# A wavelet mixer and gated feed-forward on one core: gate and up handed over separately, the low half of h on GpSimd, x1 halves and 1/den moved by DMA

## The chip, the cores and the metric

The kernel runs on one core of a Trainium2 chip. The metric is the device time of one execution in microseconds (us). TensorE is called PE here, its weight loads PEld, VectorE DVE, ScalarE ACT, GpSimd POOL, and SyncE, which issues all of the kernel's DMAs, SP.

## The reference

The input is x of shape [2, 4096, 512] in f32. Two layers follow each other:

```
l, h   = two levels of depthwise 4-tap convolutions with stride 2   (analysis)
q      = elu(l2) + 1, k = q, v = l2, 16 heads of 32 channels
low    = (q @ kv) / (q @ sum(k) + 1e-6)                             (attention)
low    = two levels of repeat by 2 and depthwise 4-tap convolutions (synthesis)
r      = x + layer_norm(x + low) * gamma + beta
x1     = layer_norm(r)
h      = silu(x1 @ wg.T) * (x1 @ wu.T)      wg, wu: [1536, 512] int32 / 127
out    = layer_norm(x1 + h @ wd.T)          wd:     [512, 1536] int32 / 127
```

## The kernel before, in words

**Work and order.** A batch's 4096 tokens are taken 1024 at a time, so there are 8 iterations of 1024 tokens. The analysis of the first batch and the casting of the weights come first (about 120 us), then the synthesis and first norms of tokens 0 to 511 (`FIRST_MIX`, `FIRST_NORM`, up to 203 us), then the 8 iterations. Iterations 0 to 2 also carry the analysis of the second batch.

**The feed-forward.** An iteration has two blocks, b = 0 and 1, of 512 tokens. PE computes in f32 accuracy with f16 operands: x1 and h are split into a high and a low half in f16. In a block, k = 0 to 11 are steps of one 128-wide piece of the hidden size: `gate_up` issues 8 gate and 8 up matmuls of 512 columns into `ps_gu[k % 2]`; ACT writes silu(gate) to `gate_s` (L754); DVE multiplies it with up into `h_f` (L1070); ACT copies `h_f` to f16 `h_hi` (L758); DVE writes `h_lo = h_f - h_hi` (L1076). Then t = 0 to 3 (slots 12 to 15) are `down` for 128 tokens each: 24 matmuls into `ps_d[t % 2]` (L539, L540). DVE adds x1 into z (L1088), POOL and ACT take turns for the mean and variance (L839, L741, L816 to L821), ACT normalises (L746, semaphore `out_done`), and SP stores (L409). The product of `ps_down` may be overwritten two t later only after L1088.

**What lies beside it.** Every engine's program is a list in order, and an engine waits in that order. The table `BESIDE`, written by hand, says which steps stand in which slot (b, k), on every engine that has a part of them. On ACT the order in a slot is silu(k), the "early" steps, the copy to `h_hi`, the "late" steps (`norm1q`, `normq`, `normx`). On DVE it is L1070, the beside steps, L1076. POOL has only the beside steps in slots 0 to 11. In slots 12 to 15 POOL runs the beside steps and then the statistics of z for t; ACT runs early steps, square(t-1), late steps, normalise(t-1).

**The steps of one tile of 128 tokens**, t = 0 to 7: `xbeta` (POOL, x + beta, L790, f32, 512 wide); `norm1` (PE transposes of `s_chan`, L489; ACT copy with sum, L666; POOL mean, L795); `norm1q` (ACT square, L671; POOL L803 and L806); `norm2` (DVE L1006 and L1012; POOL mean, L810); `normq` (ACT square, L677; POOL L816, L819, L821); `normx` (ACT, x1 in f32, L683); `norm3` (four PE transposes of x1 into `ps_y`, L507; ACT writes `x1_hi`, L688; DVE writes `x1_lo`, L1020). Tiles 0 to 3 of the next iteration stand in slots (1,9) to (1,15.5), tiles 4 to 7 of this one in (0,0) to (0,11). The first gate matmul of a block waits for `x1_hi_ready` and `x1_lo_ready` of its four tiles.

**Attention.** `dens` puts q @ sum(k) for 16 heads into 16 partitions of `ps_y`; DVE adds eps and takes the reciprocal (L935, L937). `attend` for each of four channel groups multiplies a 16-partition 0/1 matrix `spread` with 1/den on PE (L473), multiplies q with kv (L474), ACT copies the spread 1/den (L661), DVE multiplies (L941).

**SP's queue.** SP issues the loads of `xt` after `norm2` (L340), the output stores in slots 12 to 15, and a few large transfers. `hold` is a wait in that queue.

The waits that tie PE to the others are, in `gate_up`:

```python
                pe.wait_ge(h_mul, NH * B + k + 1)
                for g in range(2):
...
                mm.then_inc(gu_ready, 1)
```

so that both banks of step k wait for the product of step k-2 (`h_mul` starts at 2), and ACT's silu waits for the last up matmul.

## Time and profile before

| | |
|---|---|
| median of 3 runs | 1384.56 us (1384.21 to 1386.04) |
| span of the profiled execution, first to last instruction | 1382.5 us |
| the profiled execution's own time | not given apart from its span; the runs shown are 0.1 to 0.3% longer than that span |
| PE, DVE, ACT, POOL busy | 90%, 71%, 50%, 27% of the span |
| mean granted clock of PE | 0.971 of full speed (2.4 GHz) |
| DMA | 95.2 MB, 20.8% of the 16 DMA engines' time |
| from the first gate matmul to the end | 203.0 to 1382.5 us |

How to read it: the page gives each engine's busy time. Matmuls are pipelined, so the cost of one is read from the distance between two starts in the timeline and not from its duration. Engines that are not the bottleneck may be idle at no cost; what matters is which of them PE waits for.

### The profile page before, as it was taken

To read this page: it belongs to the slowest core of one execution; us is meant where nothing else is said; L and a number is where in the kernel's file an instruction comes from. 1 tells how busy PE (TensorE), PEld (TensorE's weight loads), DVE (VectorE), ACT (ScalarE), POOL (GpSimd) and SP (SyncE) were. 2 spreads that over 40 slices of the span, in tenths; PEclk is the share of its full clock that TensorE was granted. 3 is DMA by queue.
4 is the path that set the end of the run, shared out by engine and by line. 5 is a ranking of instruction groups with operands and counts; after the bars stand their busy time and mean duration, and the time that the engine had idled before them with its cause. 6 is when DMAs were issued, how large, how long until landed. Compare 5 with 4: busy or idle time off the path is not lost.

```text
span 1382.5 us, 18903 instructions
## 1 busy us (share of the span) xinstructions
PE 1245.5 (90%) x5920; PEld 629.5 (46%) x5920; DVE 988.1 (71%) x1913; ACT 688.8 (50%) x1384; POOL 373.0 (27%) x790
## 2 busy tenths in 40 slices
PE   3997039998999989998999999999999999999998
PEld 3885025444444444444544444444444444444443
DVE  2677938988688958988489738883898478854332
ACT  2663046345753466346753466346634664365432
POOL 2001033133423044223413143304321341234101
PEclk9998559999999999999999999999999999999999
DMA  8963033000520014000500041002200130010000
GB/s 262 285 238 123 0 123 108 23 24 24 176 77 31 0 55 147 20 23 24 176 16 31 8 148 30 31 1 84 100 23 8 53 122 23 15 38 24 16 16 31
DMA packets 48465, 95.20 MB, mean 69 GB/s; under 512 B 8448, under 2 KB 25088, under 8 KB 47376
## 3 DMA queue, kind: packets, MB, share of 16 engines
q1 hardware_dynamic: 48400, 94.42, 20.8%
q8 instruction: 30, 0.49, 0.1%
q14 instruction: 35, 0.29, 0.1%
HBM read 69.21 MB, written 25.19 MB: 68 GB/s over the span
## 4 chain that ended last, share of the span: by engine, by line
DVE 29%; PE 27%; issue 22%; ACT 12%; POOL 9%; SPq 0%; DMA 0%; DVEq 0%; POOLq 0%; ACTq 0%
DVE s_chan L864 6%; DVE h_f L1070 5%; DVE low L864 5%; PE ps_down L540 3%; PE ps_down L539 3%; PE ps_gate L522 3%; PE ps_gate L523 3%; PE ps_up L523 3%; PE ps_up L522 3%; DVE hid L1076 3%; POOL rs L819 3%; DVE h_mem L864 3%; PE ps_down L572 2%; ACT junk L671 2%; DVE l L864 2%
## 5 line engine op out<-in xcount | busy, mean ns | idle before, releaser
L522 PE MATMUL ps_gate<-x_hi,w 128*128 128x512 f16 x768 | 292.4, 381 | 27.5 <-DVE h_f L1070 25.4
L539 PE MATMUL ps_down<-w,hid 128*128 128x512 f16 x768 | 292.1, 380 | 0.1
L540 PE MATMUL ps_down<-w,hid 128*128 128x512 f16 x768 | 292.1, 380 | 0.0
L523 PE MATMUL ps_gate<-x_lo,w 128*128 128x512 f16 x768 | 292.0, 380 | 0.0
L522 PE MATMUL ps_up<-x_hi,w 128*128 128x512 f16 x768 | 291.1, 379 | 0.0
L523 PE MATMUL ps_up<-x_lo,w 128*128 128x512 f16 x768 | 291.1, 379 | 0.0
L758 ACT ACTIVATE hid<-h_f 128x512 f16<-128x512 f32 x192 | 121.0, 630 | 203.2 <-DVE h_f L1070 203.2
L1070 DVE SCALAR_TENSOR_TENSOR h_f<-ps_up,gate_s 128x512 f32<-128x512 f32 x192 | 131.7, 686 | 123.7 <-ACT gate_s L754 123.1
L1076 DVE TENSOR_TENSOR hid<-h_f,hid 128x512 f16<-128x512 f32 x192 | 139.3, 725 | 57.7 <-ACT hid L758 56.8
L754 ACT ACTIVATE gate_s<-ps_gate 128x512 f32<-128x512 f32 x192 | 112.1, 584 | 70.0 <-PE ps_up L523 69.8
L522 PEld LDWEIGHTS ps_gate<-x_hi,w 128*128 128x128 f16 x768 | 75.2, 98 | 124.9 <-DVE h_f L1070 42.2
L522 PEld LDWEIGHTS ps_up<-x_hi,w 128*128 128x128 f16 x768 | 75.2, 98 | 90.8 <-issue 0.3
L523 PEld LDWEIGHTS ps_up<-x_lo,w 128*128 128x128 f16 x768 | 75.1, 98 | 90.8 <-issue 0.3
L790 POOL TENSOR_TENSOR xt<-xt,beta_b 128x512 f32<-128x512 f32 x64 | 90.1, 1429 | 97.6 <-DMA xt<-x_tok 96.8
L539 PEld LDWEIGHTS ps_down<-w,hid 128*128 128x128 f16 x768 | 75.3, 98 | 86.8 <-DVE z L1088 3.5
L540 PEld LDWEIGHTS ps_down<-w,hid 128*128 128x128 f16 x768 | 75.3, 98 | 85.2 <-issue 1.1
L864 DVE SCALAR_TENSOR_TENSOR s_chan<-low,coef,s_chan 128x512 f32<-128x512 f32 x160 | 111.5, 748 | 1.1
L523 PEld LDWEIGHTS ps_gate<-x_lo,w 128*128 128x128 f16 x768 | 75.3, 98 | 78.7 <-issue 0.8
L795 POOL TENSOR_TENSOR rs<-rs,minus_part 128x1 f32<-128x1 f32 x64 | 21.2, 331 | 324.6 <-ACT x L666 324.6
L1020 DVE TENSOR_TENSOR x_lo<-ps_y,x_hi 128x512 f16<-128x512 f32 x64 | 43.9, 687 | 85.2 <-ACT x_hi L688 85.2
L746 ACT ACTIVATE z<-z,rs 128x512 f32<-128x512 f32 x64 | 52.0, 812 | 83.3 <-POOL rs L821 83.3
L741 ACT ACTIVATE junk<-z,rs 128x512 f16<-128x512 f32 x64 | 46.0, 718 | 89.9 <-POOL rs L839 89.9
(106 smaller groups left out, 1803.8 us busy)
## 6 DMA issues: line engine op xcount, KB each, us to landing
xa<-x_chan SPq DMA_DIRECT2D x32, 515.0 KB, 5.6
xb<-x_chan SPq DMA_DIRECT2D x8, 2060.0 KB, 8.9
xt<-x_tok SPq DMA_DIRECT2D x64, 256.0 KB, 2.6
out<-z SPq DMA_DIRECT2D x64, 256.0 KB, 2.0
hid<-weights SPq DMA_DIRECT2D x12, 768.0 KB, 6.7
q_in<-q_scratch SPq DMA_DIRECT2D x8, 518.0 KB, 8.5
h_in<-h_scratch SPq DMA_DIRECT2D x8, 518.0 KB, 9.5
h_scratch<-h SPq DMA_DIRECT2D x8, 512.0 KB, 9.2
```

What stands on the lines that cost most here:

```text
L522: pe.matmul(ps_gu[k % 2][g][:, :], w, x1_hi[:, b, c, :], start=(c == 0), stop=False)
L523: mm = pe.matmul(ps_gu[k % 2][g][:, :], w, x1_lo[:, b, c, :], start=False, stop=(c == NC - 1))
L539: pe.matmul(ps_d[t % 2][:, :], h_hi[:, k, t * P:(t + 1) * P], w, start=(k == 0), stop=False)
L540: mm = pe.matmul(ps_d[t % 2][:, :], h_lo[:, k, t * P:(t + 1) * P], w, start=False, stop=(k == NH - 1))
L741: nc.scalar.activation(junk[:, :], z[:, t, :], ACT.Square, bias=rs3[:, t, 1:2], accum_out=rs3[:, t, 2:3]).then_inc(z_squares, 1)
L746: nc.scalar.activation(z[:, t, :], z[:, t, :], ACT.Identity, bias=rs3[:, t, 5:6], scale=rs3[:, t, 4:5]).then_inc(out_done, 1)
L754: nc.scalar.activation(gate_s[:, k % 2, :], ps_gu[k % 2][0][:, :], ACT.Silu, scale=WSCALE / X1_SCALE).then_inc(silu_done, 1)
L758: nc.scalar.activation(h_hi[:, k, :], h_f[:, k % 2, :], ACT.Copy).then_inc(hi_done, 1)
L790: nc.gpsimd.tensor_tensor(xt[:, t % 4, :], xt[:, t % 4, :], beta_b[:, :], ALU.add).then_inc(x_beta, 1)
L864: return V.scalar_tensor_tensor(out=acc, in0=src, scalar=coef[:, c, n:n + 1], in1=acc if add is None else add, op0=ALU.mult, op1=ALU.add)
L1070: V.scalar_tensor_tensor(out=h_f[:, k % 2, :], in0=ps_gu[k % 2][1][:, :], scalar=WSCALE * H_SCALE / X1_SCALE, in1=gate_s[:, k % 2, :], op0 ...
L1076: V.tensor_tensor(h_lo[:, k, :], h_f[:, k % 2, :], h_hi[:, k, :], ALU.subtract).then_inc(lo_done, 1)
```

## The change

Four things are changed together.

1. **Hand-overs.** Gate and up have semaphores of their own (`gate_ready`, `up_ready`). ACT's silu waits for gate alone. PE's gate matmuls of step k wait for the silu of step k-2, its up matmuls for the product of step k-2. `gate_s` is gone: silu is written to a ring of four `h_f`, and the product is formed in place.
2. **h_lo on POOL.** DVE's L1076 becomes a POOL `tensor_tensor` of f32 and f16 to f16, 128x512, in every slot 0 to 11, between POOL's early step (`norm1`) and its late ones. The silu of step k waits for `lo_done` of step k-4, and PE's `down` for `lo_done`.
3. **x1 halves by DMA.** `normx` writes the high half in f16 from x1 on ACT first, then x1; POOL subtracts (`x1_lo`, also 128x512); `norm3` is now two `dma_start_transpose` of 128x512 f16 on SP, and PE's transposes, L688 and L1020 are gone. The halves lie in the memory of `xt`, so the next load of `xt` (`reload`) waits on SP for both transposes. The step stands one to two slots earlier or later, as the table shows; on SP it is behind the store of the slot before.
4. **1/den by DMA.** `dens` writes 4 heads of each channel group to partitions 32c to 32c+3 (rows 4 to 31 are of no use), DVE takes the reciprocal over 128 partitions, SP stores `den` to DRAM, waits, and loads it with a broadcast of each row to 32 partitions for the four groups. `spread` on PE and ACT's copy L661 are gone.

```diff
+    (0, 3): [(NOW, "normx", 5), (LATE, "turn", 2), (LATE, "turn", 3), (NOW, "norm3", 4)],
+    (0, 4): [(LATE, "kv", 0), (LATE, "blocks", 0), (NOW, "norm3", 5), (NOW, "reload", 4), (NOW, "xbeta", 6),
+             (NEXT, "high1", 0)],
+    (0, 5): [(NOW, "reload", 5), (NOW, "norm1", 6), (NOW, "norm1q", 6), (NOW, "xbeta", 7)],
...
+    (0, 8): [(NOW, "normx", 7), (NOW, "norm3", 6), (NEXT, "dens", 0)],
+    (0, 9): [(NOW, "norm3", 7), (NOW, "reload", 6)],
...
+    (1, 12): [(NEXT, "normx", 1), (NEXT, "norm2", 2), (NEXT, "normq", 2), (ANA, "band2", 3), (NEXT, "norm3", 0)],
     (1, 12.5): [(NEXT, "norm1", 3), (NEXT, "norm1q", 3)],
+    (1, 13): [(NEXT, "norm3", 1), (NEXT, "reload", 0), (NEXT, "normx", 2), (NEXT, "norm2", 3), (NEXT, "normq", 3)],
+    (1, 14): [(NEXT, "norm3", 2), (NEXT, "reload", 1), (NEXT, "normx", 3)],
+    (1, 15): [(NEXT, "reload", 2), (NEXT, "norm3", 3), (NEXT, "reload", 3)],
...
 @block.sync
+            def norm3(j, batch, t):
+                b, u = t // DSUB, t % DSUB
+                if not first(j):
+                    hold(sp, up_ready, NH * (2 * j + b - 1))
+                for w, (x1_part, ready) in enumerate(((x1_hi, x1_hi_ready), (x1_lo, x1_lo_ready))):
+                    hold(sp, ready, SUBS * j + t + 1)
+                    sp.dma_start_transpose(x1_part[:, b, :, u * P:(u + 1) * P], x1_tok[:, u, w, :]
+                                           ).then_inc(x1_turned[w][u], 16)
+            def reload(j, batch, t):
...
+                for w in range(2):
+                    hold(sp, x1_turned[w][t % DSUB], 16 * (2 * j + t // DSUB + 1))
                 load_xt(j + (t + 4) // SUBS, (t + 4) % SUBS)
+            def dens(j, batch, _):
+                hold(sp, den_step, 2 * (j + 1))
+                sp.dma_start(den_dram[:, :], den[:, :]).then_inc(st_den, 16)
+                hold(sp, st_den, 16 * (j + 1))
+                for c in range(NC):
+                    rows = den_dram[c * HEAD:c * HEAD + CHUNK_HEADS, :]
+                    sp.dma_start(att[:, c, :], rows[:, None, :].to_broadcast([CHUNK_HEADS, HEAD, QW])
+                                 ).then_inc(ld_att[c], 16)
 @block.tensor
-                pe.matmul(ps_y[:, 0:QW], spread[:, c, :], den[:, :], start=True, stop=True)
...
             def gate_up(B, b, k):
-                pe.wait_ge(h_mul, NH * B + k + 1)
                 for g in range(2):
+                    pe.wait_ge((silu_done, h_mul)[g], NH * B + k + 1)
...
-                mm.then_inc(gu_ready, 1)
+                    mm.then_inc((gate_ready, up_ready)[g], 1)
 @block.scalar
             def normx(j, batch, t):
+                nc.scalar.activation(x1_tok[:, t % DSUB, 0, :], x1[:, t, :], ACT.Identity, bias=rs2[:, t, 5:6],
+                                     scale=rs2[:, t, 4:5]).then_inc(x1_hi_ready, 1)
...
-                        act.wait_ge(gu_ready, NH * B + k + 1)
-                        nc.scalar.activation(gate_s[:, k % 2, :], ps_gu[k % 2][0][:, :], ACT.Silu,
+                        act.wait_ge(gate_ready, NH * B + k + 1)
+                        act.wait_ge(lo_done, NH * B + k + 1)
+                        nc.scalar.activation(h_f[:, k % RING, :], ps_gu[k % 2][0][:, :], ACT.Silu,
...
 @block.gpsimd
+            def normx(j, batch, t):
+                n = SUBS * j + t + 1
+                pool.wait_ge(x1_ready, n)
+                pool.wait_ge(x1_hi_ready, n)
+                nc.gpsimd.tensor_tensor(x1_tok[:, t % DSUB, 1, :], x1[:, t, :], x1_tok[:, t % DSUB, 0, :],
+                                        ALU.subtract).then_inc(x1_lo_ready, 1)
...
                     for k in range(NH + DSUB):
-                        beside(b, k, i, batch, analysis, last, steps)
+                        beside(b, k, i, batch, analysis, last, early)
+                        if k < NH:
+                            pool.wait_ge(hi_done, NH * (2 * i + b) + k + 1)
+                            nc.gpsimd.tensor_tensor(h_lo[:, k, :], h_f[:, k % RING, :], h_hi[:, k, :], ALU.subtract
+                                                    ).then_inc(lo_done, 1)
+                        beside(b, k, i, batch, analysis, last, late)
 @block.vector
-                        dve.wait_ge(hi_done, n + 1)
-                        V.tensor_tensor(h_lo[:, k, :], h_f[:, k % 2, :], h_hi[:, k, :], ALU.subtract
-                                        ).then_inc(lo_done, 1)
```

## Rows read from the trace of the kernel before

**Rows 1.** The page: span and busy time, share, instructions
```profile
span 1382.5 us, 18903 instructions
...
PE 1245.5 (90%) x5920; PEld 629.5 (46%) x5920; DVE 988.1 (71%) x1913; ACT 688.8 (50%) x1384; POOL 373.0 (27%) x790
```

**Rows 2.** Windows, iterations 0 and 5: length, busy PE, PEld, DVE, ACT, POOL, clock, DMA
```profile
203.00:358.60 155.60, 147.17 (x697) 70.45 (x698) 126.38 (x246) 81.88 (x168) 47.36 (x91) 0.98 0.16 50
...
959.50:1103.90 144.40, 139.63 (x665) 66.15 (x665) 106.47 (x195) 73.77 (x152) 43.45 (x96) 1.00 0.15 51
```

**Rows 3.** Timeline of PE, a transpose and matmuls: start, duration, what
```profile
254.76 0.27 PE L507 MATMUL ps_y<-ident,x 128*128 128x128 f32 x1
254.87 0.38 PE L522 MATMUL ps_gate<-x_hi,w 128*128 128x512 f16 x1
255.09 0.38 PE L523 MATMUL ps_gate<-x_lo,w 128*128 128x512 f16 x1
```

**Rows 4.** Timeline of PE, one `attend` in iteration 5
```profile
1168.88 0.70 PE L473 MATMUL ps_y<-den,spread 16*128 16x259 f32 x2
1169.51 0.70 PE L474 MATMUL ps_x<-q_in,kv_blocks 128*128 128x259 f32 x2
```

**Rows 5.** Groups of instructions by line: busy us, mean ns, idle before, releaser
```profile
L1076 DVE TENSOR_TENSOR hid<-h_f,hid 128x512 f16<-128x512 f32 x192 | 139.3, 725 | 57.7 <-ACT hid L758 56.8
...
L790 POOL TENSOR_TENSOR xt<-xt,beta_b 128x512 f32<-128x512 f32 x64 | 90.1, 1429 | 97.6 <-DMA xt<-x_tok 96.8 <-issue 0.8
...
L1020 DVE TENSOR_TENSOR x_lo<-ps_y,x_hi 128x512 f16<-128x512 f32 x64 | 43.9, 687 | 85.2 <-ACT x_hi L688 85.2
```

**Rows 6.** Line L790 by itself: duration in ns, least, median, most
```profile
L790 POOL TENSOR_TENSOR xt<-xt,beta_b x64: 1262/1276/1858, 117.1 to 1267.3; 128x512 f32<-128x512 f32 x64
```

**Rows 7.** Timeline of POOL and DVE at the same time, iteration 6
```profile
1182.44 4.19 POOL L790 TENSOR_TENSOR xt<-xt,beta_b 128x512 f32<-128x512 f32 x3
...
1184.00 1.49 DVE L1076 TENSOR_TENSOR hid<-h_f,hid 128x512 f16<-128x512 f32 x1 [0.70 <-ACT hid L758]
```

**Rows 8.** Timeline of ACT, slots (1,9) to (1,15) of iteration 5
```profile
1070.54 0.60 ACT L754 ACTIVATE gate_s<-ps_gate 128x512 f32<-128x512 f32 x1 [0.16 <-PE ps_up L523]
...
1078.68 0.72 ACT L677 ACTIVATE junk<-x,rs 128x512 f16<-128x512 f32 x1 [1.56 <-POOL rs L810]
...
1096.91 0.80 ACT L683 ACTIVATE x<-x,rs 128x512 f32<-128x512 f32 x1
...
1101.56 0.81 ACT L746 ACTIVATE z<-z,rs 128x512 f32<-128x512 f32 x1 [1.28 <-POOL rs L821]
```

**Rows 9.** Timeline of POOL in the same slots
```profile
1077.28 0.58 POOL L803 TENSOR_SCALAR rs<-rs 128x1 f32<-128x1 f32 x1 [1.41 <-ACT junk L671]
...
1079.66 0.19 POOL L816 TENSOR_SCALAR rs<-rs 128x1 f32<-128x1 f32 x1 [1.01 <-ACT junk L677]
...
1080.56 0.19 POOL L821 TENSOR_TENSOR rs<-rs 128x1 f32<-128x1 f32 x1
```

**Rows 10.** Timeline of PE where the next block begins
```profile
1103.82 0.39 PE L522 MATMUL ps_gate<-x_hi,w 128*128 128x512 f16 x1 [0.16 <-issue]
```

**Rows 11.** Timeline of SP: start and issue time of one DMA
```profile
1110.30 0.83 SPq L337 DMA_DIRECT2D h_in<-h_scratch  x1
```

**Rows 12.** DMA issues: count, KB each, us from issue to landing
```profile
xt<-x_tok SPq DMA_DIRECT2D x64, 256.0 KB, 2.6
out<-z SPq DMA_DIRECT2D x64, 256.0 KB, 2.0
...
h_in<-h_scratch SPq DMA_DIRECT2D x8, 518.0 KB, 9.5
```

**Rows 13.** Windows: the first 3.5 us of iteration 0, PE alone
```profile
202.90:206.40 3.50, 3.46 (x9) 0.51 0.32 111
```

**Rows 14.** Timeline before iteration 0: attention, then the first gate matmul
```profile
128.24 0.43 DVE L941 TENSOR_TENSOR att<-ps_x,att 128x259 f32<-128x259 f32 x1 [2.90 <-ACT att L661]
...
202.94 0.60 PE L522 MATMUL ps_gate<-x_hi,w 128*128 128x512 f16 x1 [1.60 <-DVE x_lo L1020]
```

More of the change, by code:

```diff
@@ L117 @@
 for _s in range(DSUB + 3):
-    FIRST_NORM += [(name, _s - lag) for name, lag in (("norm2", 0), ("normq", 0), ("normx", 1), ("norm3", 3))
+    FIRST_NORM += [(name, _s - lag) for name, lag in (("norm2", 0), ("normq", 0), ("normx", 1), ("norm3", 1), ("reload", 1))
                    if 0 <= _s - lag < DSUB]
@@ L123, with mixer_ffn @@
 AHEAD = PER_BATCH + 1
-HEADS = C // HEAD
-def mixer_ffn(nc, x_tok, x_chan, taps, gamma, beta, edge, weights, identity, block_mask, head_mask, head_spread,
-              out):
+RING = 4
+CHUNK_HEADS = P // HEAD
+def mixer_ffn(nc, x_tok, x_chan, taps, gamma, beta, edge, weights, identity, block_mask, head_mask, out):
     q_dram = nc.dram_tensor("q_scratch", [P, BATCHES, NC, SEQ // 4 + 3], F32, kind="Internal").ap()
+    den_dram = nc.dram_tensor("den_scratch", [P, QW], F32, kind="Internal").ap()
     h2_dram = nc.dram_tensor("h2_scratch", [P, BATCHES, NC, SEQ // 4 + 3], F32, kind="Internal").ap()
@@ L158, in mixer_ffn @@
         kv_blocks = sb("kv_blocks", [P, NC, P])
-        z_heads = sb("z_heads", [P, NC, HEADS])
-        head_of = sb("head_of", [P, NC, HEADS])
-        spread = sb("spread", [HEADS, NC, P])
-        den = sb("den", [HEADS, QW])
+        z_heads = sb("z_heads", [P, NC, HEAD])
+        head_of = sb("head_of", [P, HEAD])
+        den = sb("den", [P, QW])
         xb = sb("xb", [P, NC, XW])
@@ L374, in next_bands @@
                 load_bands(j, batch)
-            steps = {"low1": low1, "keys": keys_store, "norm2": after_norm2, "bands": next_bands}
+            steps = {"low1": low1, "keys": keys_store, "norm3": norm3, "reload": reload, "dens": dens,
+                     "bands": next_bands}
             run = before(steps)
@@ L393, in _ @@
             before_analyses(sp, {**steps, "out1": out1, "weights": load_weights, "kv": first_bands})
-            run(FIRST_NORM, 0, 0)
+            run(FIRST_MIX + FIRST_NORM, 0, 0)
             def body(i, batch, analysis, last):
@@ L490, in norm1 @@
                 mm.then_inc(s_ready, 1)
[L492 to L510 removed]
+            steps = {"turn": turn, "kv": kv, "dens": dens, "attend": attend, "norm1": norm1}
             def gate_up(B, b, k):
                 if k == 0:
[L515 to L518 removed]
+                    for u in range(DSUB):
+                        pe.wait_ge(x1_turned[0][u], 16 * (B + 1))
+                        pe.wait_ge(x1_turned[1][u], 16 * (B + 1))
                 for g in range(2):
+                    pe.wait_ge((silu_done, h_mul)[g], NH * B + k + 1)
                     for c in range(NC):
@@ L825, in normq @@
                                 var2, rstd2, shift2)
-            steps = {"norm1": norm1, "norm1q": norm1q, "xbeta": xbeta, "norm2": norm2, "normq": normq}
-            before(steps)(FIRST_NORM, 0, 0)
+            early = {"norm1": norm1}
+            late = {"norm1q": norm1q, "xbeta": xbeta, "norm2": norm2, "normq": normq,
+                    "normx": normx}
+            before({**early, **late})(FIRST_NORM, 0, 0)
             def body(i, batch, analysis, last):
@@ L836, in body @@
                             n = DSUB * (2 * i + b) + t + 1
-                            beside(b, k + 0.5, i, batch, analysis, last, steps)
+                            beside(b, k + 0.5, i, batch, analysis, last, early)
+                            beside(b, k + 0.5, i, batch, analysis, last, late)
                             pool.wait_ge(z_done, n + 2)
@@ L934, in dens @@
                 dve.wait_ge(den_ready, j + 1)
-                V.tensor_scalar(den[:, :], ps_y[0:HEADS, 0:QW], ATTN_EPS, None, ALU.add).then_inc(den_step, 1)
+                if not first(j):
+                    dve.wait_ge(st_den, 16 * j)
+                V.tensor_scalar(den[:, :], ps_y[:, 0:QW], ATTN_EPS, None, ALU.add).then_inc(den_step, 1)
                 dve.wait_ge(den_step, 2 * j + 1)
```

129 lines of the change are left out of this document (41 added, 88 removed).

## The prediction

> **What bounds the kernel now.** I read the page's busy times first: PE is busy 90% of the span, DVE 71%, ACT 50%, POOL 27% [rows 1]. Then the windows by iteration: an iteration without analysis takes 144.4 us with PE busy 139.6, iteration 0, with analysis, 155.6 with 147.2 [rows 2]. So PE bounds the kernel, with 5 to 10 us of idle per iteration. Its cost per piece comes from distances between starts: 0.11 us for a transpose, 0.22 for a 512-column matmul [rows 3], 0.63 for the two instructions of one spread product [rows 4]. Last I read the timelines of ACT and POOL at the end of an iteration, because the change puts most of its new work into these two lists, which are in strict order. I count time there from t = 0 at 1070.4 us, where the up matmuls of slot (1,9) end (silu follows at 1070.54 [rows 8]). Tile 0's second square (L677) starts at 8.3, tile 3's x1 ends at 27.3, the z of t=2 is normalised at 32.0 [rows 8], and the next block's gate matmul starts at 33.4 [rows 10]. Half a block's norms and its z statistics thus already take nearly all the time there is.
>
> **The change, part by part.**
> - *Transposes leave PE*: 32 x 0.11 = 3.5 us per iteration. Those of tiles 0 to 3 are inside the walk below; the other 16 save 1.76 x 8 = 14 us.
> - *Spread leaves PE*: four of 0.63 per iteration in seven iterations, 18 us. ACT's copy goes as well, off the path.
> - *DVE loses* L1076 and L1020, 24 x 0.725 + 8 x 0.687 = 22.9 us per iteration [rows 5]. It isn't the bound, so this is worth only the idle of PE that late products cause.
> - *POOL gains* 24 + 8 = 32 wide subtractions per iteration. The trace has none with an f16 operand; L790 has the same form in f32, 1.27 us [rows 6]. I take that; an end below would be 0.69, L1020's time on DVE [rows 5], an end above 1.86, the longest L790 [rows 6]. 32 x 1.27 = 41 us more on a busy time of 43.5 [rows 2].
> - *POOL and DVE get in each other's way.* Where three L790 run from 1182.44 to 1186.63, the L1076 that starts among them takes 1.49 instead of about 0.69, and the three take 4.19 instead of 3.81 [rows 7]. A blocked DVE instruction thus costs 0.8 us; for 32 per iteration that is 26 us, more than the 22.9 removed, so I count no relief for DVE. The Trainium skill, "SBUF — State Buffer", section Who interferes with whom, states a rule that speaks against this part of the change: a VectorE instruction with two SBUF inputs and a GpSimd one that reads SBUF exclude each other for the whole instruction. By it DVE would stand for up to 32 x 1.27 = 41 us per iteration; 106.5 - 22.9 + 41 = 125 is still under the iteration's length, so the sum would be the same.
> - *Separate hand-overs.* The up bank may be late by 8 x 0.22 = 1.7 us more, and silu may start 1.7 us earlier. Of the 5 to 10 us of idle, I take 0.5 per iteration as gained in b = 1 (3 us in all), where only DVE's taps make PE wait; where ACT is late, below, nothing is gained.
> - *1/den by DMA* in slot (0,8) holds SP for a store and a landing of 2.0 [rows 12] before the loads; first use is in slot 13, four steps later: hidden. Tile 7's transposes queue behind it and are wanted in (1,0): hidden. Before iteration 0 there is no cover: now DVE's product comes 2.9 us after the wait begins [rows 14]; then a store and a load one after the other, landings of 2.0 and 2.6 [rows 12] and an issue of up to 0.83 each [rows 11], some 6. That is +3.
> - *First norms*: each of the four tiles has a POOL subtraction of 1.27 in the chain of squares and means, which now takes about 2.3 per tile, and the last transposes add issue and landing; the PE and DVE chain of `norm3` (194 to 202.9 us) goes. I walk it to about 205 against 202.94 [rows 14]: +2.
>
> **The walk that decides.** POOL takes `h_lo`(k) only after ACT's copy, and only then its late steps; `normq` on ACT waits for POOL's mean of the same slot, and stands before the next silu. Units: a square 0.9 [rows 8]; POOL from release to rstd 1.2, to shift 1.25 [rows 9]; each half of normx 0.8 (L683, rows 8); subtraction 1.3; a hand-over 0.1 to 0.2. The same walk without the new work gives 8.4 and 12.6 for the first two events that the trace has at 8.3 and 12.4.
> After the change: `h_lo`(10) 6.0 to 7.3, rstd of tile 1 8.6, square of tile 0 at 8.9, its shift 11.3; silu(11) 10.4; `h_lo`(11) 12.1 to 13.4. Then in POOL's order: rstd of tile 2 14.6, subtraction of tile 0 (it waits for x1, 14.4) to 15.9, square and shift of tile 1 to 18.5; x1 of tile 1 20.1, subtraction 21.5, square and shift of tile 2 24.2; tile 3's sum, square and rstd 26.8; z0 square and shift 29.5; x1 of tile 2 29.6, subtraction 31.0; tile 3 square and shift 33.7; z1 to 36.4; x1 of tile 3 36.5, subtraction 37.9; z2 square and shift 40.6, normalised 41.5.
> SP has tile 3's transposes behind the store of z2 and a reload: 42.7. Two issues and a landing follow. No row has a transposing DMA. Ends: a landing of 2.0 like `out` and nothing for the issue (44.7), or the 9.5 of h_in twice, one after the other (61.7) [rows 12]. I take 0.83 for an issue [rows 11] and 2.6 for landing [rows 12], nearest in size: 47.0. The gate matmul starts at 47.0 instead of 33.4: **+13.6**. PE finishes its own work about t = 34 (the z product of t=1 waits on DVE behind tile 3's `norm2`) and stands still some 12 us. After a pause of this kind PE runs at half clock, 1.2 GHz: the first 3.5 us of iteration 0 have a granted clock of 0.51 [rows 13], a loss of 1.7. Together +15.3 for each of the seven passages into a next iteration: **+107**.
> The Trainium skill, "VectorE: DVE Perf Modes", section The three transpose paths, gives 1309 ns for a DMA transpose of 128x128 in two bytes. An estimate from that is 5.2 us for each half, 10.5 for the pair against my 4.3, and the sum would be 7 x 6.2 = 43 us higher.
>
> *The first half of an iteration* has the same coupling in slots (0,1) to (0,3) and (0,6) to (0,8). The same walk puts silu(2), silu(3), silu(7), silu(8) so late that PE waits 0.5, 2.7, 0, 2.4 us, about 5.7 in all, against 1.5 of the 4.8 idle now [rows 2]: +4.2 in iterations 3 to 7, and I take 5.5 in iterations 0 to 2, where ACT also has the copies of `turn`: **+37**.
>
> *Sum*: 107 + 37 - 14 - 18 - 3 + 5 = **+114**. The profiled execution's span is 1382.5 [rows 1], giving 1496; the median of the runs shown is 2.1 above the span, so I predict **1498 us**.
>
> **The rivals.**
> - *A, faster: the chain is covered.* If POOL's part is hidden (the subtractions are short, or their order costs nothing), PE keeps its gains: 14 + 14 transposes, 18 spread, and some 40 of the idle of about 46 in iterations 0 to 6, 86 us. The place of tile 3's transposes behind z2's store still costs: z2 normalised 5 us after its matmuls, then 1.2 + 4.3, against 5.2 of matmuls, so 4.5 plus 1.7 of clock, 43 in all. Time: about 1341; and 1298 if that is hidden too. For it: POOL is 27% busy [rows 1]. Against: the walk reproduces the present trace. It decides where the next gate matmul starts before about t = 34.
> - *B, much slower: slow transposes.* If a pair takes 10 us or more, +43 to +100: 1541 to 1600. For it: no row shows one. Against: only one pair per iteration is in the open; the others have a slot or more.
> - *C, mild: half of the walk is absorbed.* If half the boundary and half the b = 0 stalls are hidden, -72: about 1426. DVE's or ACT's early steps could fall into waits that I counted twice.
> - *D, DVE becomes the bound* through blocking: at most 125 us per iteration of 160; it would show only in iterations 0 to 2, where DVE has 20 us more to do [rows 2], perhaps +5 each.
>
> **How the numbers follow.** Forecast (with D) 0.60, C 0.16, B 0.08, A 0.13, no change 0.03. A measurement of this kernel can tell about 0.2% (3 us) from no change. Faster 0.13, same 0.03, slower 0.84. The range takes in C and the forecast with the lower price of a transpose and the skill's: 1400 to 1565; it leaves out A, no change, and the far end of B.
>
> **What would show it.** In the windows, iterations 4 to 6 about 160 us long with PE busy some 136, and POOL over 80. In the timeline, L522 with an idle of about 12 us before each iteration's first gate matmul, put down to a DMA of x1; the granted clock near 0.5 right after. In the waits, ACT's second square waiting for POOL's mean longer than now; POOL's wide subtractions at 1.3 us, some at 1.7; DVE instructions of 1.5 us beside them. The forecast is wrong if the first gate matmul follows the last down matmul at once, or if silu(2), silu(3) and silu(8) aren't late; its size is wrong if a transpose takes far more or less than 3 us.

## The result and the profile after

The changed kernel takes 1547.32 us (median of 4 runs, 1545.35 to 1549.82) against 1384.38 (1384.12 to 1386.04) for the kernel before on the same chip: a ratio of 1.118, 95% interval 1.1165 to 1.1196. It is slower by 163 us. Predicted were 1498 us, a range of 1400 to 1565, and slower with 0.84: the sign and the range held, the size was 49 us short. All ratios in this document are of undisturbed executions: one execution each of two experiments (4481 and 1677 us) and one of the kernel before (4424 us) stood far above the others and are not in them.

The page of the kernel after, its head and the groups that changed most (busy us, mean ns, idle before and its releaser):

```profile
span 1543.5 us, 19219 instructions
...
PE 1227.9 (80%) x5600; PEld 599.5 (39%) x5600; DVE 958.0 (62%) x1659; ACT 689.3 (45%) x1352; POOL 696.9 (45%) x1046
...
L524 PE MATMUL ps_gate<-x_hi,w 128*128 128x512 f16 x768 | 308.5, 402 | 147.8 <-DMA x_lo<-xt 111.4
L835 POOL TENSOR_TENSOR hid<-h_f,hid 128x512 f16<-128x512 f32 x192 | 253.1, 1318 | 284.1 <-ACT hid L748 283.9
L1074 DVE SCALAR_TENSOR_TENSOR h_f<-ps_up,h_f 128x512 f32<-128x512 f32 x192 | 132.5, 690 | 352.8 <-PE ps_up L525 185.1
...
L871 DVE SCALAR_TENSOR_TENSOR s_chan<-low,coef,s_chan 128x512 f32<-128x512 f32 x160 | 151.7, 997 | 1.1
...
L1022 DVE SCALAR_TENSOR_TENSOR x<-x,rs,xt 128x512 f32<-128x512 f32 x64 | 84.9, 1326 | 15.7 <-POOL rs L796 14.1
```

PE has less to do than before (1245.5 us busy in [rows 1], 5920 instructions against 5600) and yet the span is 161 us longer: the loss is waiting, and matmuls at the lower granted clock (the mean of the run is 0.918, before 0.971). Two things stand out. PE waits 111.4 us for the last transpose of x1, 26.4 of it once before iteration 0. And DVE was relieved of 256 wide subtractions, 139.3 + 43.9 us [rows 5], but its busy time fell by 30 us only: it holds 153 us that no instruction of its own explains (958.0 against 988.1 - 183.2 = 804.9). Two groups that the change does not touch show it. The taps of `s_chan` take 997 ns on average and L1022 takes 1326; in the trace of before they are these rows:

```profile
L864 DVE SCALAR_TENSOR_TENSOR s_chan<-low,coef,s_chan 128x512 f32<-128x512 f32 x160 | 111.5, 748 | 1.1
...
L1012 DVE SCALAR_TENSOR_TENSOR x<-x,rs,xt 128x512 f32<-128x512 f32 x64 | 48.1, 752 | 5.5 <-POOL rs L806 3.3
```

The windows of the kernel after: iteration 0, the two halves of iteration 5, the end of its second half, and the first 3.8 us of iteration 6 (busy PE, PEld, DVE, ACT, POOL, then clock, DMA share and GB/s), against [rows 2]:

```profile
207.05:382.90 175.85, 144.57 (x656) 66.54 (x657) 129.29 (x216) 85.29 (x167) 89.78 (x128) 0.93 0.29 75
1070.30:1148.60 78.30, 71.11 (x317) 31.73 (x318) 53.72 (x83) 35.76 (x72) 40.77 (x59) 0.93 0.34 89
1148.60:1237.30 88.70, 67.36 (x310) 30.87 (x309) 49.52 (x80) 38.08 (x76) 44.37 (x70) 0.93 0.13 35
1226.00:1237.00 11.00, 0.00 (x0) 0.00 (x0) 0.00 (x0) 3.88 (x8) 3.30 (x9) 0.59 0.71 179
1237.20:1241.00 3.80, 3.79 (x9) 1.31 (x10) 0.00 (x0) 0.16 (x1) 0.00 (x0) 0.50 0.69 194
```

The granted clock is low not only at the passage. One stretch of the first half of iteration 5, while PE works:

```profile
1111.90:1118.70 6.80, 5.85 (x14) 2.09 (x15) 4.24 (x9) 4.23 (x9) 4.05 (x8) 0.50 0.14 29
```

In the 7.9 us before this stretch PE was busy for 5.04: from 1109.04 to 1112.85 it waits for a silu.

The same two halves of iteration 5 before:

```profile
959.46:1030.86 71.40, 70.56 (x337) 33.53 (x338) 56.18 (x102) 37.17 (x77) 22.26 (x47) 1.00 0.20 71
1030.86:1103.87 73.01, 69.08 (x330) 32.63 (x329) 50.30 (x94) 36.59 (x75) 21.19 (x50) 1.00 0.10 31
```

The first half is 6.9 us longer, the second 15.7. Taken so for all iterations, from one first gate matmul to the next, the difference of the two spans falls into three parts: 4.1 us before iteration 0 (its first gate matmul stands at 207.05, before at 202.94), **44 us in the eight first halves**, and **113 us in the seven second halves** that end in a passage to a next iteration.

The timeline of PE in iteration 5 shows the three longest waits of such a second half: for the synthesis on DVE in slot (1,9), for a z product, and at the passage (start, us, what, idle before and releaser):

```profile
1191.08 1.11 PE L507 MATMUL ps_x<-ident,s_chan 128*128 128x128 f32 x4 [2.95 <-DVE s_chan L871]
...
1219.30 0.39 PE L541 MATMUL ps_down<-w,hid 128*128 128x512 f16 x1 [2.47 <-DVE z L1086]
...
1237.21 0.60 PE L524 MATMUL ps_gate<-x_hi,w 128*128 128x512 f16 x1 [12.56 <-DMA x_lo<-xt]
```

The up matmuls of slot (1,9) end at 1188.0 here. From there to the next gate matmul it is 49.2 us; before it was 33.4 [rows 10], predicted were 47.0.

What holds up the transposes is to be seen in the timeline of SP at that passage (start and time of each issue):

```profile
1207.62 1.20 SPq L352 DMA_TRANSPOSE x_lo<-xt  x1
1223.30 0.34 SPq L433 DMA_DIRECT2D out<-z  x1
1223.87 1.20 SPq L352 DMA_TRANSPOSE x_hi<-xt  x1
1225.15 1.21 SPq L352 DMA_TRANSPOSE x_lo<-xt  x1
1226.77 0.36 SPq L343 DMA_DIRECT2D xt<-x_tok  x1
1227.45 0.33 SPq L433 DMA_DIRECT2D out<-z  x1
1228.01 1.23 SPq L352 DMA_TRANSPOSE x_hi<-xt  x1
1229.33 1.22 SPq L352 DMA_TRANSPOSE x_lo<-xt  x1
...
1232.74 1.19 SPq L352 DMA_TRANSPOSE x_hi<-xt  x1
1234.03 1.22 SPq L352 DMA_TRANSPOSE x_lo<-xt  x1
```

Tile 1's low half was ready at 1213.0 (below), but its transposes are issued at 1223.87, behind the store of z tile 0; from then on SP issues almost without a pause.

The timeline of DVE and of POOL in slots (1,8) and (1,9), where the synthesis becomes late:

```profile
1184.51 6.44 DVE L871 SCALAR_TENSOR_TENSOR s_chan<-low,coef,s_chan 128x512 f32<-128x512 f32 x5
```

```profile
1183.46 1.16 POOL L835 TENSOR_TENSOR hid<-h_f,hid 128x512 f16<-128x512 f32 x1 [2.68 <-ACT hid L748]
1184.58 1.80 POOL L780 TENSOR_TENSOR xt<-xt,beta_b 128x512 f32<-128x512 f32 x1
1186.34 1.60 POOL L835 TENSOR_TENSOR hid<-h_f,hid 128x512 f16<-128x512 f32 x1
1187.91 1.70 POOL L780 TENSOR_TENSOR xt<-xt,beta_b 128x512 f32<-128x512 f32 x1
...
1211.88 1.15 POOL L802 TENSOR_TENSOR xt<-x,xt 128x512 f16<-128x512 f32 x1 [1.63 <-ACT x L680]
```

Five taps take 6.44 us here and 3.52 in the trace of before (at 1064.99), while POOL has four wide instructions in a row: two L835, two L780. The lock, as I call it from here on, works both ways: an L835 takes 1.16 us free and 1.60 here. L780 is not new: it adds beta to x, and for tiles 0 to 3 its slots in the table are the same. In the trace of before the four of them ran one behind the other already at 1036.79, for 5.41 us, because nothing held POOL; now POOL's list waits for ACT in every slot, and they fall beside the taps.

### The profile page after: what moved, and what is told of

It reads as the page before. It is cut to its first block, busy times and chain, and to the rows that moved or that the text cites. A ratio compares the mean times of both kernels' runs of the same rounds, so it can differ in the third digit from the quotient of the medians.

```text
span 1543.5 us, 19219 instructions
## 1 busy us (share of the span) xinstructions
PE 1227.9 (80%) x5600; PEld 599.5 (39%) x5600; DVE 958.0 (62%) x1659; ACT 689.3 (45%) x1352; POOL 696.9 (45%) x1046
## 2 busy tenths in 40 slices
DMA packets 123445, 117.27 MB, mean 76 GB/s; under 512 B 78320, under 2 KB 100080, under 8 KB 122352
## 4 chain that ended last, share of the span: by engine, by line
issue 27%; DVE 21%; POOL 19%; PE 14%; ACT 13%; SPq 2%; DMA 2%; POOLq 0%; DVEq 0%; ACTq 0%
DVE s_chan L871 8%; POOL hid L835 4%; DVE low L871 4%; POOL xt L802 4%; DVE h_f L1074 3%; POOL rs L816 2%; ACT h_f L744 2%; DVE h_mem L871 2%; PE ps_down L574 2%; ACT xt L678 2%; PE ps_gate L524 2%; PE ps_gate L525 2%; PE ps_up L524 2%; ACT x L680 2%; ACT junk L730 2%
## 5 line engine op out<-in xcount | busy, mean ns | idle before, releaser
L524 PE MATMUL ps_gate<-x_hi,w 128*128 128x512 f16 x768 | 308.5, 402 | 147.8 <-DMA x_lo<-xt 111.4
L835 POOL TENSOR_TENSOR hid<-h_f,hid 128x512 f16<-128x512 f32 x192 | 253.1, 1318 | 284.1 <-ACT hid L748 283.9
L1074 DVE SCALAR_TENSOR_TENSOR h_f<-ps_up,h_f 128x512 f32<-128x512 f32 x192 | 132.5, 690 | 352.8 <-PE ps_up L525 185.1
L525 PE MATMUL ps_gate<-x_lo,w 128*128 128x512 f16 x768 | 308.0, 401 | 0.0
L871 DVE SCALAR_TENSOR_TENSOR s_chan<-low,coef,s_chan 128x512 f32<-128x512 f32 x160 | 151.7, 997 | 1.1
L780 POOL TENSOR_TENSOR xt<-xt,beta_b 128x512 f32<-128x512 f32 x64 | 99.1, 1551 | 95.1 <-DMA xt<-x_tok 95.1
L744 ACT ACTIVATE h_f<-ps_gate 128x512 f32<-128x512 f32 x192 | 111.2, 579 | 55.4 <-PE ps_gate L525 55.4
L525 PEld LDWEIGHTS ps_gate<-x_lo,w 128*128 128x128 f16 x768 | 78.4, 102 | 88.9 <-issue 15.8
L672 ACT ACTIVATE junk<-x,rs 128x512 f16<-128x512 f32 x64 | 46.2, 722 | 121.6 <-POOL rs L807 121.6
L813 POOL TENSOR_SCALAR rs<-rs 128x1 f32<-128x1 f32 x128 | 31.1, 243 | 144.6 <-ACT junk L730 80.2
L1022 DVE SCALAR_TENSOR_TENSOR x<-x,rs,xt 128x512 f32<-128x512 f32 x64 | 84.9, 1326 | 15.7 <-POOL rs L796 14.1
## 6 DMA issues: line engine op xcount, KB each, us to landing
h_in<-h_scratch SPq DMA_DIRECT2D x8, 518.0 KB, 10.8
```

What stands on the lines that cost most here:

```text
L524: pe.matmul(ps_gu[k % 2][g][:, :], w, x1_hi[:, b, c, :], start=(c == 0), stop=False)
L525: mm = pe.matmul(ps_gu[k % 2][g][:, :], w, x1_lo[:, b, c, :], start=False, stop=(c == NC - 1))
L744: nc.scalar.activation(h_f[:, k % RING, :], ps_gu[k % 2][0][:, :], ACT.Silu, scale=WSCALE / X1_SCALE).then_inc(silu_done, 1)
L780: nc.gpsimd.tensor_tensor(xt[:, t % 4, :], xt[:, t % 4, :], beta_b[:, :], ALU.add).then_inc(x_beta, 1)
L835: nc.gpsimd.tensor_tensor(h_lo[:, k, :], h_f[:, k % RING, :], h_hi[:, k, :], ALU.subtract).then_inc(lo_done, 1)
L871: return V.scalar_tensor_tensor(out=acc, in0=src, scalar=coef[:, c, n:n + 1], in1=acc if add is None else add, op0=ALU.mult, op1=ALU.add)
```

## The experiments

Three suspects come out of these views: **the lock** between POOL's wide subtractions and DVE; **POOL's place in the chain**, that is the subtractions delaying everything behind them in POOL's list, which is the prediction's walk; and **SP's queue**. Each run below takes one of them away. Times are medians; the kernel before had 1384.2, 1383.9, 1384.2 and 1383.2 us in the four sessions.

### h_lo back on DVE

```diff
 # POOL, before its late steps
-    nc.gpsimd.tensor_tensor(h_lo[:, k, :], h_f[:, k % RING, :], h_hi[:, k, :], ALU.subtract)
 # DVE, after the steps of the slot
+    V.tensor_tensor(h_lo[:, k, :], h_f[:, k % RING, :], h_hi[:, k, :], ALU.subtract)
```

> The changed kernel with h_lo back on DVE behind the product (as before the change), x1_lo still on POOL. Chain theory (POOL's ordered list lengthens the ACT-POOL chain of the norms): POOL no longer waits for ACT's copy in slots 0 to 11, so the waits of the first half (some 7 us per iteration) go and the gate matmul of the next iteration comes some 4 us earlier; 7 x 11 = 77 us less, about 1470 us. Port theory (DVE blocked by POOL's reads is the cost): DVE gets its 139 us of subtractions back and loses three quarters of the blocking; PE's waits for late taps (some 6 us per iteration) go, 7 x 6 = 42 less, about 1505 us. SP theory (the order on SP's queue and the transposes are the cost): no more than 10 us less.

Measured: 1487.78 us, ratio 1.0752 (1.0734 to 1.0769), 60 us less than the changed kernel. It lies between the two figures. The taps of `s_chan` are back to 747 ns.

### The x1 subtraction on DVE

```diff
-    # POOL: normx
-    nc.gpsimd.tensor_tensor(x1_tok[:, t % DSUB, 1, :], x1[:, t, :], x1_tok[:, t % DSUB, 0, :], ALU.subtract)
+    # DVE: norm3, in the slot that BESIDE gives it
+    V.tensor_tensor(x1_tok[:, t % DSUB, 1, :], x1[:, t, :], x1_tok[:, t % DSUB, 0, :], ALU.subtract)
```

> The changed kernel with the x1_lo subtraction moved from POOL's normx to DVE in the slot of norm3, h_lo still on POOL. Chain theory: POOL's four subtractions and its waits for x1 leave the chain at the end of the iteration (about 8 us earlier at the next gate matmul) and two slots of the first half (4 to 5 us); 7 x 12.5 = 87 less, about 1460 us. Port theory: only 8 of 32 wide POOL reads per iteration go, 10 us less, about 1537 us. SP theory: unchanged, 1547 us.

Measured: 1506.21 us, ratio 1.0867 (1.0844 to 1.0889), 41 us less: again in between. Eight subtractions per iteration are worth two thirds of what 24 are worth, so these eight cost by where they stand, and the 24 by something else.

### h_lo without its reads

```diff
-    nc.gpsimd.tensor_tensor(h_lo[:, k, :], h_f[:, k % RING, :], h_hi[:, k, :], ALU.subtract)
+    nc.gpsimd.memset(spare[:, :], 0.0)
+    nc.gpsimd.memset(h_lo[:, k, :], 0.0)
```

> The changed kernel, but in each slot 0 to 11 POOL writes zeros instead of reading h_f and h_hi: one memset of a spare tile and one of h_lo, both 128x512 f16 (it leaves out the low half of h). POOL is then occupied for about as long at the same place of its list, but reads nothing. Chain theory: the time stays as far as the two memsets take what the subtraction took (1.2 to 1.6 us); about 1535 us, within 1520 to 1547. Port theory: DVE's instructions are no longer stretched (997 ns back to 748 for the synthesis taps), 42 us or more less, 1505 us or below.

Measured: 1473.06 us, ratio 1.0632 (1.0611 to 1.0654), **74 us less**, though POOL still waits for ACT in the same place and is occupied for 1.05 us there instead of 1.16. The groups of this run:

```profile
L874 DVE SCALAR_TENSOR_TENSOR s_chan<-low,coef,s_chan 128x512 f32<-128x512 f32 x160 | 133.2, 882 | 1.1
L839 POOL MEMSET hid<- 128x512 f16 x192 | 101.1, 526 | 0.0
L838 POOL MEMSET spare<- 128x512 f16 x192 | 100.8, 525 | 285.3 <-ACT hid L749 283.7
```

The expectation that POOL's place decides (1535) falls; the lock is the larger part. DVE is busy 870.0 us instead of 958.0. It is not free of the lock, though: its taps still take 882 ns on average, against 747 in the run with h_lo on DVE. Five of them, and POOL beside them:

```profile
1125.01 5.61 DVE L874 SCALAR_TENSOR_TENSOR s_chan<-low,coef,s_chan 128x512 f32<-128x512 f32 x5
```

```profile
1125.02 1.27 POOL L782 TENSOR_TENSOR xt<-xt,beta_b 128x512 f32<-128x512 f32 x1
...
1127.17 1.45 POOL L782 TENSOR_TENSOR xt<-xt,beta_b 128x512 f32<-128x512 f32 x1
```

Taps of `s_chan` that ran beside memsets alone took 0.74 to 0.75 us (21 of 160), those beside L782 alone 1.75 to 1.76 (14). So the 74 us are the reads of h_lo, and what the lock costs through the old additions, moved beside the taps by POOL's place in its list, is not in them.

In block 11 (second half of iteration 5) the distance from the first gate matmul to the end of the up matmuls of slot (1,9) is 35.4 us instead of 39.5, and from there to the next gate matmul 47.1 instead of 49.2: 6.2 us, times seven 44, and the second halves together are 45 us shorter. The first halves give 29.

### Both without their reads, and both on DVE

Both subtractions as memsets:

```diff
+    nc.gpsimd.memset(x1_tok[:, t % DSUB, 1, :], 0.0)    # twice, in place of the subtraction in normx
```

> The changed kernel with both new POOL subtractions replaced by two memsets of 128x512 f16 each, 0.53 us a piece in e3's trace, at the same places (it leaves out the low halves of h and of x1). No new POOL reads are left, the places in POOL's list are as in the changed kernel. Port theory: the last 8 of 32 reads per iteration are worth a quarter of e3's gain, 15 to 25 us: about 1453 us. The distance from here to e5 is then what POOL's place in the chain costs: 60 to 80 us by the forecast's walk. If that distance is under 15 us, the chain theory falls and the reads were all.

Measured: 1470.19 us, ratio 1.0616 (1.0596 to 1.0637): 3 us less than with h_lo alone, within the two intervals. The reads of the x1 subtraction cost nothing that can be told. Both subtractions on DVE, the two edits above together:

> The changed kernel with both subtractions on DVE (h_lo in slots 0 to 11, x1_lo in the slot of norm3); separate hand-overs, x1 halves and 1/den by DMA stay. If POOL's part (its place in the list and the reads together) explains all that the DMAs do not, what is left is SP's order and the transposes: z2 normalised at about 32 us as before the change, then 12.5 us to the gate matmul as in the trace of e1 (here 38 to 40), 5.5 + 1.7 of clock per iteration, 50 in all, against gains of some 14 + 18 + 3 for PE and 30 of its idle: about 1375, between 1360 and 1400 us. If the transposes cost more than POOL's part, above 1450 us.

Measured: 1438.85 us, ratio 1.0391 (1.0369 to 1.0412). Against the run with memsets POOL's time in its list is gone as well, and that is worth 31 us, half of what was expected. The 31 are a net sum: the taps no longer meet the additions (748 ns), but DVE has the subtractions to do (998.0 us busy against 862.7). The waits of this run hold the rest:

```profile
PE ps_gate L524 <- DMA x_lo<-xt: 100.2, 8, 25.5
```

(25.5 of it is before iteration 0.) The next gate matmul comes 40.6 us after the up matmuls of slot (1,9), not 33.4 as before, though the x1 halves of tile 3 are ready at 30.1. With POOL cleared, 55 us over the kernel before were left, and my expectation of 1375 was wrong by 64.

### SP's order

First only tile 3's transposes, moved ahead of tile 2's reload and of the store of z tile 2, on the changed kernel and on the one with both subtractions on DVE:

```diff
-    (1, 14): [(NEXT, "norm3", 2), (NEXT, "reload", 1), (NEXT, "normx", 3)],
-    (1, 15): [(NEXT, "reload", 2), (NEXT, "norm3", 3), (NEXT, "reload", 3)],
+    (1, 14): [(NEXT, "norm3", 2), (NEXT, "reload", 1), (NEXT, "normx", 3), (NEXT, "norm3", 3)],
+    (1, 15): [(NEXT, "reload", 2), (NEXT, "reload", 3)],
```

> The changed kernel with one entry of the table moved: norm3 of tile 3 stands at the end of slot (1,14), so SP issues its two transposes before it waits for the store of z2. Chain theory with SP's order as a part of it: x1_lo of tile 3 is ready at 39.4 us after the up matmuls of slot (1,9), SP now issues at 46.0 to 47.3; the gate matmul at about 42.5 to 43.5 instead of 49.2, 7 x 6 = 42 less, 1505 us. If SP's order costs nothing because another thing is as late (the transposes of tile 2, the ACT chain), 1545 us.

Measured: 1528.11 us, ratio 1.1033 (1.1015 to 1.1052), 19 us less, half of the way.

> e5 with tile 3's norm3 at the end of slot (1,14), ahead of the store of z2 on SP. If SP's order is on the path there: 3 to 4 us less per iteration, 20 to 28 less than e5. If the path is the ordered chain before it: no difference to e5.

Measured: 1424.95 us, ratio 1.0292 (1.0273 to 1.0311), 14 us less, short of the 20 expected. Then the four stores of the second half behind all transposes (and, in the same edit, the reload of tile 1 ahead of tile 2's transposes; the two were not tried apart):

```diff
+    (1, 14): [(NEXT, "reload", 1), (NEXT, "norm3", 2), (NEXT, "normx", 3), (NEXT, "norm3", 3)],
+    (1, 15): [(NEXT, "reload", 2), (NEXT, "reload", 3)],
 # SP
-    if k >= NH:                       # store z tile k - NH
+    # b == 0: as before; b == 1: the four stores after the last slot
```

> Edit: the run with both subtractions on DVE and tile 3's transposes issued in slot (1,14), and on SP the four output stores of the second half are issued after all transposes and reloads of the passage instead of between them. In the trace of the run without this edit tile 1's halves are ready 18.8 us after the up matmuls of slot (1,9), but SP issues their transposes only at 28.4 us, behind the store of z tile 0, which waits until 27.0; eight transposes, four stores and two reloads of 1.3 us then follow each other and the next gate matmul comes at 38.7 us. Theory that SP's queue is what is left of the loss at the passage: tiles 0 to 2 are then out of the way by 27 us, tile 3's last half is ready at 30.1, issued by 31.4 and landed by 34, the next gate matmul comes at 34 to 35 us as before the change, and the time falls by 4 us x 7 and some clock, from 1425 to about 1393. Rival that the transposes' own time in the DMA queues is what is left (each 128 x 512 half 2.5 us, one after another): no more than 10 us less, 1415 or above.

Measured: **1391.01 us** (1388.99 to 1394.39), ratio 1.005 (1.0036 to 1.0063), 34 us less, as expected by the theory of SP's queue. Two timelines show what moved. SP in the kernel with both subtractions on DVE, where the up matmuls of slot (1,9) end at 1109.4:

```profile
1135.94 0.34 SPq L433 DMA_DIRECT2D out<-z  x1
1136.51 1.20 SPq L352 DMA_TRANSPOSE x_hi<-xt  x1
...
1146.97 1.22 SPq L352 DMA_TRANSPOSE x_lo<-xt  x1
```

and in the one with the stores last, where they end at 1077.6:

```profile
1095.00 1.19 SPq L352 DMA_TRANSPOSE x_hi<-xt  x1
...
1107.77 1.19 SPq L352 DMA_TRANSPOSE x_lo<-xt  x1
...
1111.24 3.65 SPq L434 DMA_DIRECT2D out<-z  x4
```

Tile 1's transposes start 17.4 us after the up matmuls instead of 27.1, because SP no longer stands in front of a store whose z is not there yet; the last starts at 30.2 instead of 37.6. PE at the same passage:

```profile
1110.62 0.39 PE L525 MATMUL ps_gate<-x_hi,w 128*128 128x512 f16 x1 [3.42 <-DMA x_lo<-xt]
```

The wait at the passage is 3.4 us, where it was 0.16 before the change [rows 10], and the distance is 33.0, where it was 33.4. Last, the same order on the changed kernel, with both subtractions left on POOL:

> Edit: the changed kernel with nothing but SP's order altered: tile 3's transposes in slot (1,14), reload of tile 1 ahead of tile 2's transposes, and the four output stores of the second half behind all of them; both subtractions stay on GpSimd. With the subtractions on VectorE the same order was worth 48 us (1439 to 1391). Theory that SP's queue and GpSimd's place in the chain are taken one behind the other: in the changed kernel's trace the last x1_lo half is subtracted at 39.3 us after the up matmuls of slot (1,9), so with an empty queue its transpose is issued by 40.6 and landed by 43.2, the next gate matmul comes at 43.5 instead of 49.2, 5.7 us x 7 = 40 us less, about 1507. Rival that the late subtraction alone decides and the queue only fills the time before it: no more than the 19 us that tile 3's order gave, 1525 or above.

Measured: 1502.12 us, ratio 1.0861 (1.0845 to 1.0876), 45 us less. The queue costs 45 us with the subtractions on POOL and 48 (1439 to 1391) without: the terms are taken one behind the other, as the first theory said. In block 11 the distance falls from 49.2 to 42.1. The wait for x_lo falls from 111.4 to this:

```profile
PE ps_gate L525 <- DMA x_lo<-xt: 64.5, 8, 26.3
```

### The parts that should gain

Two runs put the helpful parts alone on the kernel before. The separate hand-overs:

```diff
-    pe.wait_ge(h_mul, NH * B + k + 1)
     for g in range(2):
+        pe.wait_ge((silu_done, h_mul)[g], NH * B + k + 1)
...
-    mm.then_inc(gu_ready, 1)
+        mm.then_inc((gate_ready, up_ready)[g], 1)
```

> The kernel before with the separate hand-overs of gate and up alone. The forecast's view: PE's idle for late products is about half of its 5 to 10 us per iteration and the tolerance of 1.7 us covers most single waits (1.4 us at most): 15 to 30 us less, about 1362 us. The rival: DVE is late by the sum of its taps, so the wait only moves from the gate to the up bank: under 5 us less.

Measured: 1377.78 us, ratio 0.995 (0.9931 to 0.9968): 6 us faster. And with 1/den by DMA as well (its parts of the diff, with x1 left on TensorE):

> Edit: the kernel before, with the separate hand-overs and with 1/den spread by DMA instead of by TensorE and ScalarE; x1 turned by TensorE and both subtractions on DVE as before. Theory, with the prediction's own price of this part: 4 spread matmuls of TensorE and 4 copies of ScalarE an iteration gone, -18 us, and +3 us in the prologue for the store and the loads: from 1378 with the hand-overs alone to about 1363. Rival: the spread matmuls and the copies lay beside other work (TensorE's stalls only move to the next wait), or the loads of 1/den queue behind other issues of SP: within 5 us of 1378.

Measured: **1376.02 us** (1374.29 to 1376.45), ratio 0.9933 (0.992 to 0.9946), the best of all kernels here, and 2 us beside the hand-overs alone, with intervals that overlap: the rival, not my price. PE's busy time and its waits before and after this step, from the two runs:

```profile
PE 1245.6 (91%) x5920; PEld 630.2 (46%) x5920; DVE 989.0 (72%) x1914; ACT 684.8 (50%) x1384; POOL 368.2 (27%) x790
```

```profile
PE 1210.2 (88%) x5856; PEld 616.2 (45%) x5856; DVE 988.0 (72%) x1914; ACT 674.9 (49%) x1352; POOL 371.0 (27%) x790
```

```profile
PE ps_up L528 <- DVE h_f L1075: 13.8, 14, 1.4
PE ps_gate L528 <- ACT gate_s L754: 13.8, 18, 1.2
```

```profile
PE ps_up L523 <- DVE h_f L1074: 4.4, 7, 0.9
PE ps_gate L523 <- ACT gate_s L756: 2.6, 3, 0.9
```

The first of these two pairs is of the run with 1/den by DMA, the second of the one with the hand-overs alone. PE does 35.4 us less work and the time falls by 2; in place of the work stand waits for the silu and the product of the slot, 27.6 us against 7.0, and more waiting for the products of the attention (21.7 us, against 14.7 for it and for `den`) and for z (10.8 against 4.9).

## Why the prediction was right or wrong

*What it had right.* At the passage ACT and POOL hand work to each other in strict order and SP takes tile 3's transposes behind the store of z tile 2. The walk gave the events of this chain in the second half of an iteration; measured, in us after the up matmuls of slot (1,9):

| event | predicted | measured |
|---|---|---|
| subtraction of tile 0 / 1 / 2 / 3 | 15.9 / 21.5 / 31.0 / 37.9 | 19.6 / 25.1 / 33.4 / 39.3 |
| z tile 2 normalised | 41.5 | 42.4 |
| first issue of tile 3 | 42.7 | 44.7 |
| from there to the gate matmul | 4.3 | 4.5 |
| next gate matmul | 47.0 | 49.2 |

PE stands still for 12.6 us there (predicted 12), and the first 3.8 us after it have a granted clock of 0.50, the lower of its two levels (1.2 GHz), as the prediction had it from [rows 13]. The passages were to cost 15.3 us each, 107 in all, 13.6 of it by the distance. The distance grew by 15.8 in block 11 and by 112 in all seven. With h_lo's reads left out it is 47.1, the walk's own figure; the walk had no lock in it. Of the first half it had 5.7 us of PE's waiting; in iteration 5 three waits there make 6.6 (1.53 before the gate matmuls of k = 5, 3.81 before those of k = 9, 1.22 before the up matmuls of k = 7), the longest not where the walk had it.

*Where it was wrong.* The prediction's sum, laid out by place, against the distances between the matmuls (in us, all iterations):

| place | predicted | measured |
|---|---|---|
| before iteration 0 | 5 | 4 |
| second halves up to slot (1,9) | -12 (half of the spread, hand-overs) | 1 |
| up matmuls of (1,9) to next gate, seven | 95 | 112 |
| first slot of a first half (clock) | 12 | 16 |
| the rest of the first halves | 14 (37 - 14 - half of the spread) | 28 |
| sum | 114 | 161 |

The 47 us between the spans (1543.5 against 1496) come mainly from the two steps below, and in some part from a third; the exact shares no run gives.

1. **The gains of PE, 14 + 18 + 3 = 35 us, did not come.** The step was "the other 16 save 1.76 x 8 = 14 us" and "four of 0.63 per iteration in seven iterations, 18 us", taken from PE's busy time as if PE were the bound wherever it works. It is not: in the slots PE waits for the silu and the product of two slots earlier, and work taken from it leaves a wait. In the seven second halves slots (1,1) and (1,3) to (1,5) are 23 us shorter, and slot (1,6), where PE waits for DVE's products, gives 18 of them back. On the kernel before, where nothing else is in the way, the spread was worth 2 us and not 18. The hand-overs were worth 6 there, more than the 3 that I took, but in the changed kernel nothing of either is left: the distance from the first gate matmul of block 11 to the end of the up matmuls of slot (1,9) is 39.5 us in both, and 37.8 with the hand-overs alone on the kernel before. With h_lo's reads left out, and no subtraction of h_lo on DVE either, it is 35.4: 4.1 less, 29 us in seven, more than the 12 that I had there. So the gain is there where DVE is free, and DVE's time takes it. The 14 of the transposes were not tried by themselves; the run with the stores last, free of lock and queue, has its first halves 9 us longer than before, not shorter, though their first slots, in part at the lower clock, account for 10 by themselves.
2. **The lock was priced on DVE and not on PE.** The step was "A blocked DVE instruction thus costs 0.8 us; for 32 per iteration that is 26 us, more than the 22.9 removed, so I count no relief for DVE." The sum of DVE was good: 153 / 8 = 19 us per iteration measured. The conclusion that it costs the kernel nothing was not. The blocked instructions are the taps and norms in front of PE: the synthesis ends late (2.95 us of wait in slot (1,9)), so tile 0's chain begins later (its subtraction at 19.6, not 15.9) and the next gate matmul with it. This gives 2.2 us of the 15.8, 15 in seven passages, and the prediction named none of it. The two steps are not apart from each other: part of the gains that did not come is this lock.
3. **The clock was counted at the passages alone**, 1.7 us each. PE's 5600 instructions are busy for 1227.9 us here and for 1191.8 in the run with both subtractions on DVE, which has the same ones: 36 us more, at a mean granted clock of 0.918 against 0.940. Such stretches of 0.50 stand inside the halves too, as the one at 1111.90 above. How much of the 36 lengthens the span, and how much only fills waits, no run parts.

*What it could not have told.* The runs say how large each suspect is: reads of h_lo 74 us, of x1's low half 3, POOL's time in its list 31, SP's order 14 + 34; with them gone the kernel stands at 1391. They are steps in this order, and the reads of h_lo are only a part of the lock. This differs from the prediction's account, which laid 107 + 37 to the coupling of ACT and POOL with SP's store and reload at its end. The walk was right in its times, but it gave one chain with several causes in it: at the passage 7.1 us of the 15.8 were SP's queue (49.2 to 42.1), which can be had back by an order, and the first halves' 37 were the lock as much as the coupling (29 us of the 74 lie there). Where a walk's end comes out right, the share of each step is still to be tested.

*The skill's two rules.* An L835 that starts free takes 1.16 us and one that finds DVE at work up to 1.72; a tap takes 0.75 or up to 1.77 (line L871, shortest and longest 739 and 1769 ns), not much less than a whole subtraction more. By the Trainium skill, "SBUF — State Buffer", section Who interferes with whom, the two exclude each other for the whole instruction: the trace agrees, though only part of the 32 instructions per iteration meet one of DVE's (19 us, not 41). Instructions of DVE that read PSUM for one operand are not held here: L1074 takes 690 ns here and 686 before (L1070). The other rule was the one of the Trainium skill, "VectorE: DVE Perf Modes", section The three transpose paths; the estimate made from it was 10.5 us for a pair of halves. Measured from the first issue to the gate matmul are 4.5, so scaling the figure by the width does not hold for 128x512 in one DMA; the measurement decides. The page's own case, 128x128, no run here shows.

*The rivals.* A (covered chain, 1341 or 1298) fell: PE waits 12.6 us at the passage, and no kernel here comes below 1374. B (slow transposes) fell with the 4.5 us. C (half absorbed) fell. Of D the half about iterations 0 to 2 held in part: their second halves lose 16 to 18 us, the later ones 15 to 16. The first halves go the other way: iterations 0 to 2, which were to lose more, lose 4 to 5 us, iterations 3 to 6 5 to 7.

## What to carry to other kernels

A queue in strict order is a resource of its own: before a step is added to it, list what stands in front, and ask of each whether it waits for something later than the new step does. Here stores that waited for z held six transposes of each passage, most of them with their data there; the order was worth 45 to 48 us. Wide GpSimd instructions that read SBUF were paid twice here, on GpSimd and on the VectorE instructions with both operands in SBUF that they met, and a wait put into GpSimd's list also moved old wide instructions beside new neighbours; look at what these feed, not at VectorE's busy share. And work taken from an engine that is 90% busy gains only where that engine, and not a hand-over, sets the pace of the slot: look for its waits in the same slots first.
